# A feed-forward phase in 16 groups of two tiles instead of 8 groups of four

## The chip, the cores and the metric

One core of one Trainium2 chip. The number is the device time of one execution of the whole kernel in microseconds, the median of the runs shown; lower is better. Engine names: PE is TensorE (PEld its weight loads), DVE VectorE, ACT ScalarE, POOL GpSimd, SP SyncE.

## What is computed

The kernel is a two-layer perceiver block on x of 64 x 64 rows of 256 numbers. It has six sub-layers, each added to x: cross-attention with biases, a polynomial self-attention, a mixture of experts, a second cross-attention, a softmax self-attention, and last the feed-forward that is changed here. Cut to that one:

```python
def act_quant(x):            # one scale for each row
    scale = 127.0 / clip(max(abs(x), axis=-1), 1e-5)
    return clip(round(x * scale), -128, 127) / scale
# weight_quant: one scale for the matrix, values -1, 0, 1
h = act_quant(layernorm(x)) @ weight_quant(w1).T    # 256 -> 1024
h = depthwise_conv1d(h, conv_w, conv_b)             # 3 taps over the 64 rows of a sequence
h = silu(h)
x = x + act_quant(h) @ weight_quant(w2).T           # 1024 -> 256
```

## The kernel before, in words

X, the running sum, stays in SBUF as 32 tiles of 128 rows (two sequences of 64 rows each). The sub-layers are phases one behind another, each a block of five instruction streams, one for each engine, tied by counting semaphores. `feed_forward` (L2012) is the last but the output transfer.

It works on groups of G = 4 tiles, W = 512 columns, n = 8 groups. Its stream on each engine is `step(s, par)`, run by `tile_steps` for s = 0 to n + 3: steps 0 to 3 are written out, the middle ones are a loop of two steps a turn with counters in registers, the last four are written out. One step does pieces of five groups at once, in eight slots f = 0 to 7, one for each block of 128 hidden features:

- group s: statistics (L2177, L2181), 1/std on POOL (L2099, L2101), xn (L2187), its greatest absolute value and the scale (L2193 to L2201), rounding to xr (L2270), transposition (L2327) and xqT (L2243), and back_b, the scale spread over all partitions by a matmul with diagonal matrices (L2275, L2333, L2247).
- group s-1: for each f two bf16 matmuls w1 x xqT (L2296) into ps_h, h (L2152) on DVE, two float32 matmuls with diagonal matrices for the outer taps (L2304) into ps_y one slot later, y with the middle tap (L2160) two slots later, SiLU on ACT (L2252) three slots later. In f = 7 the peak over the first four feature blocks (L2169).
- group s-2: in f = 3 the peak over the other four and the maximum of both (L2169, L2174), four transposes of it (L2312), in f = 4 the greatest value of each row and scale2 (L2206 to L2214), four diagonals diag2 (L2264), in f = 5 the matmul L2318, in f = 6 scale_b (L2238). From there POOL multiplies (L2107) and rounds (L2115) y.
- group s-3: hq in bf16 on ACT (L2258).
- group s-4: the output matmuls (L2342), for each tile eight of 256 columns into ps_o[i % 2], and the update of X (L2219). PE does tiles 0 and 1 in f = 0 and tiles 2 and 3 in f = 1; before tile i it waits until X has been updated for tile i-2, since the buffer is the same (L2339). DVE updates tiles 0 and 1 in f = 1, 2 and 3 in f = 2.

Every engine works strictly in the order of its stream, so a wait holds up all that is written behind it. The order is written by hand. The PSUM buffers ps_h, ps_y and ps_o are double; ps_x and ps_b are single and serve two groups each in a step.

Of the kernel before, what the change touches and what calls it, by code (L numbers as in the profile page):

```python
# [28 lines left out]
ALU = mybir.AluOpType  # L29
# [1982 lines left out]
def feed_forward(nc, c, X, d):  # L2012
# [7 lines left out]

    G, n, F = 4, NT // 4, 1024
    FC = F // P
    W = G * P
    with ExitStack() as ctx:
# [93 lines left out]
        def _(dve):  # L2120
# [21 lines left out]
            def step(s, par):  # L2142
                q, last = s - 2, s - 4
                for f in range(FC):
                    g = s - 1
                    if live(g, n):

                        if f == 0:
                            dve.wait_ge(back_ready, g + 1)
                        dve.wait_ge(h_done, FC * g + f + 1)  # L2150
                        wait(dve, taps_done, FC * g + f - 3)
                        V.tensor_tensor(h[:, f % 4, :, 1:T + 1], ps_h[f % 2][:, :].rearrange("p (b t) -> p b t", t=T),  # L2152
                                        back_b[:, 1 - par, :].rearrange("p (b t) -> p b t", t=T), ALU.mult)\
                            .then_inc(h_ready, 1)
                    g, j = unit(s, f, 2)
                    if live(g, n):
                        yp = (par + 1 + (f < 2)) % 2
                        dve.wait_ge(taps_done, FC * g + j + 1)
                        wait(dve, hq_ready, FC * (g - 2) + j + 1)
                        V.scalar_tensor_tensor(y[:, yp, j, :].rearrange("p (b t) -> p b t", t=T),  # L2160
                                               h[:, j % 4, :, 1:T + 1], cw[:, j, 1:2],
                                               ps_y[j % 2][:, :].rearrange("p (b t) -> p b t", t=T),
                                               ALU.mult, ALU.add).then_inc(y_ready, 1)
                    g, half = (s - 1, 0) if f == 7 else (q, 1)
                    if f in (3, 7) and live(g, n):
# [37 lines left out]
                    if f == 4 and live(q, n):  # L2203
                        dve.wait_ge(peak_done, q + 1)
                        wait(dve, diag2_ready, q)
                        V.tensor_reduce(top2[:, :], ps_x[:, :].rearrange("p (i c) -> p i c", i=G), AX.X, ALU.max)\  # L2206
                            .then_inc(top2_ready, 1)
                        dve.wait_ge(top2_ready, 3 * q + 1)
                        V.tensor_scalar(top2[:, :], top2[:, :], 1e-5, None, ALU.max).then_inc(top2_ready, 1)
                        dve.wait_ge(top2_ready, 3 * q + 2)  # L2210
                        V.reciprocal(scale2[:, :], top2[:, :]).then_inc(top2_ready, 1)
                        dve.wait_ge(top2_ready, 3 * q + 3)
                        V.tensor_scalar(scale2[:, :], scale2[:, :], 127.0, None, ALU.mult)
                        V.tensor_scalar(back2[:, par, :], top2[:, :], w_mean[:, 1:2], 1.0 / 127, ALU.mult, ALU.mult)\  # L2214
                            .then_inc(scale2_ready, 1)
                    if f in (1, 2) and live(last, n):
                        for i in (2 * f - 2, 2 * f - 1):
                            dve.wait_ge(o_done, G * last + i + 1)
                            V.scalar_tensor_tensor(X[:, last * G + i, :], ps_o[i % 2][:, 0:E], back2[:, par, i:i + 1],  # L2219
                                                   X[:, last * G + i, :], ALU.mult, ALU.add).then_inc(x_updated, 1)  # L2220
            tile_steps(dve, step, n=n, lag=4)

        @block.scalar
        def _(act):
            act.wait_ge(consts_set, 4)
            act.wait_ge(loaded, 16 * n_loads)
            for i, t in enumerate((0, 2)):
                for j in range(FC):
                    ins = nc.scalar.activation(tap[:, i, j, :], c.ident[:, :], ACT.Copy, scale=cw[:, j, t:t + 1])
            ins.then_inc(tap_set, 1)  # L2230

            def step(s, par):
                q = s - 2
                for f in range(FC):
                    if f == 6 and live(q, n):
                        act.wait_ge(scale_done, q + 1)
                        wait(act, scaled, FC * (q - 1))
                        nc.scalar.activation(scale_b[:, par, :], ps_b[:, :], ACT.Copy).then_inc(scale_ready, 1)  # L2238
                    if f == 6 and live(s, n):
                        wait(act, h_done, FC * (s - 1))  # L2240
                        for k in range(KC):
                            act.wait_ge(xT_done, KC * s + k + 1)
                            nc.scalar.activation(xqT[:, par, k, :], ps_x[:, :], ACT.Identity,  # L2243
                                                 bias=rounding[:, 1:2]).then_inc(xqT_ready, 1)
                        act.wait_ge(back_done, s + 1)
                        wait(act, h_ready, FC * (s - 1))
                        nc.scalar.activation(back_b[:, par, :], ps_b[:, :], ACT.Copy).then_inc(back_ready, 1)  # L2247
# [12 lines left out]
                    if f == 4 and live(q, n):  # L2260
                        act.wait_ge(scale2_ready, q + 1)
                        wait(act, scale_done, q)
                        for i in range(G):
                            ins = nc.scalar.activation(diag2[:, i, :], c.ident[:, :], ACT.Copy, scale=scale2[:, i:i + 1])  # L2264
                        ins.then_inc(diag2_ready, 1)
                    if f == 5 and live(s, n):
                        act.wait_ge(scale1_ready, s + 1)
                        wait(act, xT_done, KC * s)
                        for i in range(G):
                            ins = nc.scalar.activation(xr[:, i, :], xn[:, i, :], ACT.Identity, bias=rounding[:, 0:1],  # L2270
                                                       scale=scale1[:, i:i + 1])
                        ins.then_inc(xr_ready, 1)
                        wait(act, back_done, s)
                        for i in range(G):
                            ins = nc.scalar.activation(diag1[:, i, :], c.ident[:, :], ACT.Copy, scale=back1[:, i:i + 1])  # L2275
                        ins.then_inc(diag1_ready, 1)
            tile_steps(act, step, n=n, lag=4)

        @block.tensor
        def _(pe):  # L2280
# [6 lines left out]
            def step(s, par):  # L2287
                q, last = s - 2, s - 4
                for f in range(FC):
                    g = s - 1  # L2290
                    if live(g, n):
# [1 line left out]
                            pe.wait_ge(xqT_ready, KC * g + KC)  # L2293
                        wait(pe, h_ready, FC * g + f - 1)
                        for k in range(KC):
                            mm = nc.tensor.matmul(ps_h[f % 2][:, :], w1[:, k, f * P:(f + 1) * P],  # L2296
                                                  xqT[:, 1 - par, k, :], start=(k == 0), stop=(k == KC - 1))
                        mm.then_inc(h_done, 1)
                    g, j = unit(s, f, 1)
                    if live(g, n):  # L2300
                        pe.wait_ge(h_ready, FC * g + j + 1)
                        wait(pe, y_ready, FC * g + j - 1)
                        for i in range(2):
                            mm = nc.tensor.matmul(ps_y[j % 2][:, :], tap[:, i, j, :],  # L2304
                                                  h[:, j % 4, :, 2 * i:2 * i + T], start=(i == 0), stop=(i == 1))
                        mm.then_inc(taps_done, 1)
                    if f == 3 and live(q, n):
# [7 lines left out]
                    if f == 5 and live(q, n):  # L2315
                        pe.wait_ge(diag2_ready, q + 1)
                        pe.wait_ge(back_ready, q + 2 if not isinstance(q, int) else min(n, q + 2))
                        nc.tensor.matmul(ps_b[:, :], ones[:, :], diag2[:, :, :].rearrange("p i t -> p (i t)"),  # L2318
                                         start=True, stop=True).then_inc(scale_done, 1)
                    if f == 6 and live(s, n):  # L2320
                        pe.wait_ge(xr_ready, s + 1)
# [11 lines left out]
                        nc.tensor.matmul(ps_b[:, :], ones[:, :], diag1[:, :, :].rearrange("p i t -> p (i t)"),  # L2333
                                         start=True, stop=True).then_inc(back_done, 1)
                    if f < 2 and live(last, n):
                        pe.wait_ge(hq_ready, FC * last + FC)
                        for i in (2 * f, 2 * f + 1):
                            if isinstance(s, int) or f == 1:
                                wait(pe, x_updated, G * last + i - 1)  # L2339

# [133 lines left out]
```

## Time and profile before

| | us |
|---|---|
| median of 3 runs | 2681.48 (2681.24 to 2689.95) |
| the profiled execution | 2684.85 |
| its span | 2683.1 |
| feed-forward, first statistics to last update of X | 318.2 |
| mean granted clock of PE over the span | 0.915 |

Over the whole span PE is busy 82%, DVE 56%, ACT 38% and POOL 34%. A row of the timeline reads: start, length, engine, line, operation, output<-inputs, sizes, how often, and in brackets how long the engine stood idle before it and who released it. "f32 x4" are four instructions merged. A row of the stages reads: stretch, its length, busy time of PE, PEld, DVE, ACT and POOL with the number of instructions, the mean clock that PE was granted as a share of full speed, the DMA share and GB/s. A row of the groups reads: line, engine, operation, sizes, count | busy us, mean ns of one | idle time before and who ended it.

### The profile page before, as it was taken

What the parts mean: (1) busy time and instruction counts of PE and PEld (TensorE: products, weight loads), DVE (VectorE), ACT (ScalarE), POOL (GpSimd) and SP (SyncE); (2) the same over time, 40 slices, a digit from 0 to 9 for tenths busy, and PEclk for the clock granted to TensorE, in tenths of its full rate; (3) what the DMA queues carried; (4) which work ended last, traced back from release to release, by engine and by line L of the source; (5) the groups of instructions that cost most, each with busy time, mean ns of one, the idle gap of its engine ahead of it and who ended that gap; (6) DMA issues with size and microseconds to landing.
All of it is one profiled execution on the core that took longest, in us unless ns stands there. A gap on an engine that the chain in (4) does not pass through costs nothing. (4 is left out here: it accounts for less than half of the span.)

```text
span 2683.1 us, 58677 instructions
## 1 busy us (share of the span) xinstructions
PE 2207.0 (82%) x19450; PEld 1620.2 (60%) x19463; DVE 1490.4 (56%) x4214; ACT 1012.8 (38%) x2135; POOL 900.2 (34%) x1082
## 2 busy tenths in 40 slices
PE   4999999999789963399999999976776888567774
PEld 4777777777679963156555555545555777533332
DVE  4666666666566657422233333326664777567763
ACT  3665666566444410011122222212223555334442
POOL 3444444444211112377000000017763333205555
PEclk9999999999888875699999999998997999878986
DMA  3000001000033311454122222225541000100001
GB/s 119 29 27 26 26 26 34 28 26 26 17 115 98 98 37 37 166 185 172 51 76 76 78 76 77 77 99 149 162 144 23 9 8 8 37 0 1 0 0 63
DMA packets 164872, 168.38 MB, mean 63 GB/s; under 512 B 81841, under 2 KB 139954, under 8 KB 163506
## 3 DMA queue, kind: packets, MB, share of 16 engines
q1 hardware_dynamic: 124162, 83.27, 10.7%
q0 software_dynamic: 17152, 52.45, 5.9%
q10 hardware_dynamic: 23472, 31.54, 3.4%
q8 instruction: 51, 0.84, 0.1%
q14 instruction: 35, 0.29, 0.0%
HBM read 100.09 MB, written 62.91 MB: 61 GB/s over the span
## 5 line engine op out<-in xcount | busy, mean ns | idle before, releaser
L1921 POOL DMA_INDIRECT xb_expert_y<-expert_outs,moe_slot x128 | 125.7, 982 | 561.3 <-POOLq L76 526.1
L1812 PE MATMUL ex_ps_h<-moew_w,ex_xT 128*128 x576 | 287.5, 622 | 20.7 <-DVE ex_xT L1870 9.8
L427 ACT ACTIVATE xa_prob<-xa_neg_s,xa_neg_max 128x256 f32<-128x256 f32 x512 | 224.4, 499 | 130.3 <-DVE xa_neg_max L314 130.3
L1865 DVE TENSOR_TENSOR ex_g<-ex_act_g,ex_ps_h 128x256 f32<-128x256 f32 x144 | 60.7, 421 | 311.4 <-ACT ex_act_g L1845 311.4
L314 DVE CUSTOM_DVE_ANT_0 xa_neg_s<-xa_ps_s,xa_mask 128x256 f32<-128x256 f32 x512 | 191.1, 421 | 39.0 <-PE xa_ps_s L481 24.9
L434 ACT ACTIVATE xa_probT<-xa_ps_s 128x512 f32<-128x512 f32 x256 | 151.9, 593 | 58.5 <-PE xa_ps_s L492 57.0
L510 PE MATMUL xa_ps_o<-xa_v,xa_probT 128*64 128x34 f32 x4096 | 172.9, 229 | 0.2 <-ACT xa_probT L434 0.2
L1812 PEld LDWEIGHTS ex_ps_h<-moew_w,ex_xT 128*128 128x128 f32 x576 | 98.0, 190 | 123.8 <-issue 123.8
L510 PEld LDWEIGHTS xa_ps_o<-xa_v,xa_probT 128*64 128x64 f32 x4096 | 143.9, 140 | 47.8 <-issue 40.0
L492 PE MATMUL xa_ps_s<-g_ident,xa_prob 128*128 128x128 f32 x1024 | 163.9, 283 | 2.8 <-ACT xa_prob L427 2.4
L1845 ACT ACTIVATE ex_act_g<-ex_ps_h 128x256 f32<-128x256 f32 x144 | 55.2, 383 | 293.9 <-PE ex_ps_h L1812 293.9
L1826 PE MATMUL ex_ps_y<-moew_w,ex_gT 128*128 x576 | 148.4, 380 | 1.2 <-DVE ex_gT L1875 1.2
L270 POOL TENSOR_TENSOR xa_qz<-xa_q,xa_in_pair 128x256 fp32r<-128x256 f32 x128 | 74.5, 613 | 197.5 <-DVE xa_q L362 197.5
L1676 POOL DMA_INDIRECT expert_rows<-sh_xn,sh_idx x128 | 123.1, 962 | 51.3 <-issue 38.5
L2304 PE MATMUL ff_ps_y<-ff_h,ff_tap 128*128 128x512 f32 x256 | 133.2, 647 | 7.4 <-DVE ff_y L2160 7.4
L492 PEld LDWEIGHTS xa_ps_s<-g_ident,xa_prob 128*128 128x128 f32 x1024 | 112.5, 141 | 10.9 <-ACT xa_prob L427 3.7
L1945 PE MATMUL xb_ps_g<-xb_ctx_rows 128*128 128x256 f32 x512 | 117.8, 384 | 0.0
L2107 POOL TENSOR_TENSOR ff_y<-ff_y,ff_scale_b 128x512 f32<-128x512 f32 x64 | 82.2, 1286 | 101.9 <-ACT ff_scale_b L2238 101.9
L1080 POOL TENSOR_TENSOR sa_shifted<-sa_masked,sa_top 128x512 f32<-128x512 f32 x64 | 68.1, 1064 | 125.6 <-DVE sa_top L1099 125.6
L1826 PEld LDWEIGHTS ex_ps_y<-moew_w,ex_gT 128*128 128x128 f32 x576 | 98.3, 190 | 9.6 <-issue 2.1
L1945 PEld LDWEIGHTS xb_ps_g<-xb_ctx_rows 128*128 128x128 f32 x512 | 95.9, 192 | 12.6 <-issue 0.4
L1849 ACT ACTIVATE ex_y<-ex_ps_y 128x256 f32<-128x256 f32 x144 | 55.2, 383 | 105.5 <-PE ex_ps_y L1826 105.5
(298 smaller groups left out, 4911.7 us busy)
## 6 DMA issues: line engine op xcount, KB each, us to landing
expert_rows<-sa_zero POOLq DMA_DIRECT2D x16, 1152.0 KB, 5.6
ex_xg<-expert_rows SPq DMA_DIRECT2D x144, 128.0 KB, 2.0
expert_outs<-ex_y ACTq DMA_DIRECT2D x144, 128.0 KB, 1.7
xa_ctxT<-in_ctxT_dram SPq DMA_DIRECT2D x32, 512.0 KB, 3.5
xb_ctx_rows<-in_ctx_rows_dram SPq DMA_DIRECT2D x32, 512.0 KB, 4.1
moew_w<-in_moe_w_dram ACTq DMA_DIRECT2D x8, 1024.0 KB, 5.5
g_x<-in_x_dram SPq DMA_DIRECT2D x4, 1024.0 KB, 9.9
sa_v<-sa_vs SPq DMA_DIRECT2D x128, 32.0 KB, 2.2
```

The source lines that it names most:

```text
L314: ins = nc.vector.tensor_tensor_reduce(neg_s[:, u % 2, g, :], ps_s[j][:, g * S:(g + 1) * S], mask[:, b, :], -1.0, 3e38, ALU.add, ALU.min, ...
L427: ins = nc.scalar.activation(prob[:, u % 2, i, :], neg_s[:, u % 2, i, :], ACT.Exp, bias=neg_max[:, u % 2, i:i + 1], scale=-1.0)
L434: nc.scalar.activation(probT[:, u % 2, :, :, :].rearrange("p i c t -> p (i c t)"), ps_s[u % 4][:, :], ACT.Copy).then_inc(t_ready, 1)
L492: mm = nc.tensor.transpose(ps_s[u % 4][:, k:k + P], prob[:, u % 2, g, ch * P:(ch + 1) * P], c.ident[:, :])
L510: mm = nc.tensor.matmul(ps_o[b][rows, q * 2 * D1:(q + 1) * 2 * D1], probT[:, u % 2, g, ch, rows], v[:, ap, 2 * b + ch, 2 * q:2 * q + 2, :] ...
L1676: nc.gpsimd.indirect_dma_start(c.xg_dram[:, :], bass.IndirectOffsetOnAxis(ap=idx[:, par, TOP * i + k:TOP * i + k + 1], axis=0), xn[:, par, ...
L1812: mm = nc.tensor.matmul(ps_h[1 - par][:, :], xT[:, 1 - par, k, :], c.w1[:, own, k, :], start=(k == 0), stop=(k == KC - 1))
L1826: mm = nc.tensor.matmul(ps_y[1 - par][:, 0:E], gT[:, 1 - par, k, :], c.w2[:, own, k, :], start=(k == 0), stop=(k == KC - 1))
L1921: nc.gpsimd.indirect_dma_start(expert_y[:, s % 4, k, :], None, c.y_dram[:, :], bass.IndirectOffsetOnAxis(ap=c.slot[:, s, k:k + 1], axis=0))\
L1945: mm = nc.tensor.matmul(ps_g[q % 2][b][:, g * E:(g + 1) * E], ctx_rows[:, q, 2 * b + k, g * P:(g + 1) * P], ctx_rows[:, q, 2 * b + k, :], ...
L2107: nc.gpsimd.tensor_tensor(y[:, gp, j, :], y[:, gp, j, :], scale_b[:, gp, :], ALU.mult)\
L2304: mm = nc.tensor.matmul(ps_y[j % 2][:, :], tap[:, i, j, :], h[:, j % 4, :, 2 * i:2 * i + T], start=(i == 0), stop=(i == 1))
```

## The change

G becomes 2 and n becomes 16: W is 256 columns, and all tiles of SBUF follow W. The PSUM tiles stay 512 wide, and only their first W columns are used. One output tile is made in f = 0 and one in f = 1 (i = f), and DVE updates X for tile 0 in f = 1 and tile 1 in f = 2 (i = f - 1). The slots, their order, the semaphores and the waits' formulas stay. There are 20 steps instead of 12: four written out, a loop of six turns of two steps instead of two turns, four written out. Nothing is changed outside `feed_forward`.

```diff
-    G, n, F = 4, NT // 4, 1024
+    G, n, F = 2, NT // 2, 1024
...
-                        V.tensor_tensor(h[:, f % 4, :, 1:T + 1], ps_h[f % 2][:, :].rearrange("p (b t) -> p b t", t=T),
+                        V.tensor_tensor(h[:, f % 4, :, 1:T + 1], ps_h[f % 2][:, 0:W].rearrange("p (b t) -> p b t", t=T),
...
                     if f in (1, 2) and live(last, n):
-                        for i in (2 * f - 2, 2 * f - 1):
+                        for i in (f - 1,):
                             dve.wait_ge(o_done, G * last + i + 1)
...
                     if f < 2 and live(last, n):
                         pe.wait_ge(hq_ready, FC * last + FC)
-                        for i in (2 * f, 2 * f + 1):
+                        for i in (f,):
                             if isinstance(s, int) or f == 1:
                                 wait(pe, x_updated, G * last + i - 1)
```

The other edits put `0:W` in place of `:` for ps_y in L2160 and L2304, ps_x in L2206 and L2243, ps_b in L2238, L2247, L2318 and L2333, and ps_h in L2296.

## Rows read from the trace of the kernel before

**Rows 1.** The page, part 4: the chain that ended last, by line

```profile
PE ff_ps_y L2304 1%; DVE ff_peak L2169 1%; PE ff_ps_h L2296 1%; DVE ff_y L2160 1%; PE ff_ps_o L2342 1%; ACT ff_xr L2270 0%; POOL ff_y L2107 0%; DVE ff_h L2152 0%; DVE ff_top L2193 0%; POOL ff_y L2115 0%; PE ff_ps_b L2333 0%; PE ff_ps_x L2312 0%; PE ff_ps_b L2318 0%; DVE ff_stats L2177 0%; PE ff_ps_x L2327 0%
```

**Rows 2.** Busy time by stretch of the feed-forward: fill, step 3, steps 4 to 8, drain

```profile
2350.13:2400.16 50.03, 33.22 (x86) 14.41 (x88) 32.70 (x67) 18.70 (x33) 3.79 (x6) 0.81 0.00 0
2400.16:2432.06 31.90, 24.32 (x63) 10.62 (x64) 24.27 (x41) 15.36 (x29) 15.05 (x15) 0.87 0.00 1
2432.06:2609.60 177.54, 135.97 (x472) 67.14 (x480) 131.58 (x217) 84.83 (x160) 97.98 (x91) 0.91 0.00 0
2609.60:2668.30 58.70, 32.51 (x135) 18.79 (x136) 24.27 (x36) 20.80 (x35) 37.09 (x33) 0.72 0.00 0
```

**Rows 3.** Timeline of two neighbouring steps, 2454 to 2486 us

```profile
2454.63 0.70 DVE L2152 TENSOR_TENSOR ff_h<-ff_ps_h,ff_back_b 128x512 f32<-128x512 f32 x1
2455.23 0.76 DVE L2160 SCALAR_TENSOR_TENSOR ff_y<-ff_h,ff_cw,ff_ps_y 128x512 f32<-128x512 f32 x1
...
2459.26 1.92 PE L2342 MATMUL ff_ps_o<-ff_w,ff_hq 128*128 128x256 bf16 x16 [1.18 <-DVE g_x L2219]
...
2461.74 0.69 DVE L2152 TENSOR_TENSOR ff_h<-ff_ps_h,ff_back_b 128x512 f32<-128x512 f32 x1 [2.14 <-PE ff_ps_h L2296]
...
2468.79 1.05 DVE L2174 TENSOR_TENSOR ff_peak<-ff_peak 128x512 f32<-128x512 f32 x1
...
2471.97 0.69 DVE L2152 TENSOR_TENSOR ff_h<-ff_ps_h,ff_back_b 128x512 f32<-128x512 f32 x1 [0.84 <-PE ff_ps_h L2296]
...
2476.58 1.28 ACT L2264 ACTIVATE ff_diag<-g_ident,ff_scale 128x128 f32<-128x128 f32 x4 [10.06 <-DVE ff_back L2214]
...
2477.91 1.13 PE L2318 MATMUL ff_ps_b<-ff_diag,ff_ones 128*128 128x512 f32 x2 [0.39 <-ACT ff_diag L2264]
...
2485.31 0.69 DVE L2152 TENSOR_TENSOR ff_h<-ff_ps_h,ff_back_b 128x512 f32<-128x512 f32 x1 [4.45 <-PE ff_ps_h L2296]
```

**Rows 4.** The chain in order of time: start, length, what

```profile
2504.43 1.06 DVE ff_peak L2174
...
2520.58 1.72 PE ff_ps_y L2304 x4
```

**Rows 5.** Timeline of DVE in the first cross-attention, 256-wide instructions

```profile
505.57 0.42 DVE L314 CUSTOM_DVE_ANT_0 xa_neg_s<-xa_ps_s,xa_mask 128x256 f32<-128x256 f32 x1
...
505.91 0.42 DVE L314 CUSTOM_DVE_ANT_0 xa_neg_s<-xa_ps_s,xa_mask 128x256 f32<-128x256 f32 x1
```

**Rows 6.** Groups of instructions by shape, feed-forward

```profile
L2169 DVE TENSOR_REDUCE ff_peak<-ff_y 128x512 f32<-128x2048 f32 x16 | 59.6, 3725 | 0.0
...
L2252 ACT ACTIVATE ff_y<-ff_y,ff_cb 128x512 f32<-128x512 f32 x64 | 45.6, 716 | 61.5 <-DVE ff_y L2160 61.5
...
L2193 DVE TENSOR_REDUCE ff_top<-ff_xn 128x4 f32<-128x1024 f32 x8 | 9.7, 1213 | 0.0
```

**Rows 7.** Groups of instructions by shape, other phases, 256 columns

```profile
L1945 PE MATMUL xb_ps_g<-xb_ctx_rows 128*128 128x256 f32 x512 | 117.8, 384 | 0.0
...
L1845 ACT ACTIVATE ex_act_g<-ex_ps_h 128x256 f32<-128x256 f32 x144 | 55.2, 383 | 293.9 <-PE ex_ps_h L1812 293.9
```

**Rows 8.** The chain in order of time, POOL's last pairs: first, and what follows them

```profile
2642.29 1.26 POOL ff_y L2107
...
2660.08 1.01 POOLq L2026
```

**Rows 9.** Busy time by stretch: two at low clock, one idle in the gram phase

```profile
2390.00:2393.00 3.00, 3.00 (x6) 1.23 (x5) 1.98 (x8) 0.72 (x1) 1.13 (x2) 0.50 0.00 0
2468.60:2475.20 6.60, 5.23 (x11) 2.55 (x12) 5.62 (x14) 0.00 (x0) 0.69 (x1) 0.50 0.00 0
1904.24:1906.00 1.76, 0.00 (x1) 0.01 (x1) 1.09 (x4) 0.00 (x0) 1.28 (x3) 1.00 0.84 179
```

**Rows 10.** Who waited for whom in the feed-forward: us, times, longest

```profile
PE ff_ps_x L2312 <- DVE ff_peak L2174: 36.3, 8, 5.6
```

**Rows 11.** Timeline of PE, the tap matmuls before that low stretch

```profile
2389.00 2.83 PE L2304 MATMUL ff_ps_y<-ff_h,ff_tap 128*128 128x512 f32 x4 [2.08 <-DVE ff_y L2160]
```

More of the change, by code:

```diff
@@ L2161, in step @@
                                                h[:, j % 4, :, 1:T + 1], cw[:, j, 1:2],
-                                               ps_y[j % 2][:, :].rearrange("p (b t) -> p b t", t=T),
+                                               ps_y[j % 2][:, 0:W].rearrange("p (b t) -> p b t", t=T),
                                                ALU.mult, ALU.add).then_inc(y_ready, 1)
@@ L2205, in step @@
                         wait(dve, diag2_ready, q)
-                        V.tensor_reduce(top2[:, :], ps_x[:, :].rearrange("p (i c) -> p i c", i=G), AX.X, ALU.max)\
+                        V.tensor_reduce(top2[:, :], ps_x[:, 0:W].rearrange("p (i c) -> p i c", i=G), AX.X, ALU.max)\
                             .then_inc(top2_ready, 1)
@@ L2237, in step @@
                         wait(act, scaled, FC * (q - 1))
-                        nc.scalar.activation(scale_b[:, par, :], ps_b[:, :], ACT.Copy).then_inc(scale_ready, 1)
+                        nc.scalar.activation(scale_b[:, par, :], ps_b[:, 0:W], ACT.Copy).then_inc(scale_ready, 1)
                     if f == 6 and live(s, n):
@@ L2242, in step @@
                             act.wait_ge(xT_done, KC * s + k + 1)
-                            nc.scalar.activation(xqT[:, par, k, :], ps_x[:, :], ACT.Identity,
+                            nc.scalar.activation(xqT[:, par, k, :], ps_x[:, 0:W], ACT.Identity,
                                                  bias=rounding[:, 1:2]).then_inc(xqT_ready, 1)
@@ L2246, in step @@
                         wait(act, h_ready, FC * (s - 1))
-                        nc.scalar.activation(back_b[:, par, :], ps_b[:, :], ACT.Copy).then_inc(back_ready, 1)
+                        nc.scalar.activation(back_b[:, par, :], ps_b[:, 0:W], ACT.Copy).then_inc(back_ready, 1)
                     g, j = unit(s, f, 3)
@@ L2295, in step @@
                         for k in range(KC):
-                            mm = nc.tensor.matmul(ps_h[f % 2][:, :], w1[:, k, f * P:(f + 1) * P],
+                            mm = nc.tensor.matmul(ps_h[f % 2][:, 0:W], w1[:, k, f * P:(f + 1) * P],
                                                   xqT[:, 1 - par, k, :], start=(k == 0), stop=(k == KC - 1))
@@ L2303, in step @@
                         for i in range(2):
-                            mm = nc.tensor.matmul(ps_y[j % 2][:, :], tap[:, i, j, :],
+                            mm = nc.tensor.matmul(ps_y[j % 2][:, 0:W], tap[:, i, j, :],
                                                   h[:, j % 4, :, 2 * i:2 * i + T], start=(i == 0), stop=(i == 1))
@@ L2317, in step @@
                         pe.wait_ge(back_ready, q + 2 if not isinstance(q, int) else min(n, q + 2))
-                        nc.tensor.matmul(ps_b[:, :], ones[:, :], diag2[:, :, :].rearrange("p i t -> p (i t)"),
+                        nc.tensor.matmul(ps_b[:, 0:W], ones[:, :], diag2[:, :, :].rearrange("p i t -> p (i t)"),
                                          start=True, stop=True).then_inc(scale_done, 1)
@@ L2332, in step @@
                         wait(pe, back_ready, s)
-                        nc.tensor.matmul(ps_b[:, :], ones[:, :], diag1[:, :, :].rearrange("p i t -> p (i t)"),
+                        nc.tensor.matmul(ps_b[:, 0:W], ones[:, :], diag1[:, :, :].rearrange("p i t -> p (i t)"),
                                          start=True, stop=True).then_inc(back_done, 1)
```

## The prediction

> **What bounds the kernel now.** I read the page's chain first [rows 1]: the work that ended last runs through the feed-forward, and no single engine carries it. PE's tap matmuls (L2304), DVE's peak reduction (L2169), PE's L2296 and DVE's L2160 share it. The change touches this phase only, so I take the phase's own clock: from its first statistics at 2350.13 us to its last update of X at 2668.3, 318.2 us of the profiled span.
>
> Next I cut that stretch at the ends of the peak reduction of f=3 [rows 2]: 50.0 us until step 2's, 31.9 for step 3, 177.5 for five more steps (35.5 each), 58.7 of drain. 318.2 less eight steps of 35.5 is 34: all that filling and draining cost beyond eight full steps. In each of the five steps PE is busy 27.2 us, DVE 26.3, POOL 19.6, ACT 17.0. Nobody is full; the step is a ring of hand-overs.
>
> The timeline of a loop step shows the ring [rows 3]. I count from one start of L2174 (2468.79) to the next (2504.43 [rows 4]), 35.64 us, in three parts:
> - A, 9.12 us, to the scale matmul L2318 (2477.91). The reader should see L2174, then four transposes and L2296 until the h of f=4 can start (3.18); then h, y, the top of xn, the second top and their small operations until ACT gets the scale of diag2 (4.61); then four diagonals (1.33).
> - B, 7.40 us, to the h of f=7 (2485.31): on ACT two activations, four xr, four diag1, scale_b, two xqT, with PE's transposes between, then L2333 and L2296.
> - C, the other 19.12 us, mostly DVE. Its later pieces are seen a step earlier in the rows: from h of f=0 to PE's third output tile 4.63, in which PE stood 1.18 us for g_x; from there to h of f=2 2.48, in which DVE stood 2.14 for PE; f=2, f=3 and the peak 7.05. The remainder, h, y and peak of f=7, is 4.96.
>
> **What the change does to the sum.** Twice the steps, half the columns. If a step halved exactly, 16 steps of 17.8 would cost what 8 of 35.5 do, and fill and drain would halve: 17 us gained. But every microsecond of a step that doesn't halve is paid 14 to 16 times, so the result hangs on one number, the length of the new step; break-even is about 1.1 over half.
>
> What halves: the counts of transposes, diagonals, xr, statistics, normalisations, output tiles. What has a fixed part: every instruction that stays and gets narrower. What of it is exposed comes from start-to-start times. DVE at 256 columns takes 0.42 us and the next starts after 0.34 [rows 5]; h at 512 takes 0.70 and y starts after 0.60 [rows 3]. So 256 columns are 0.27 and 0.07 stays: h 0.33, y 0.39 from start to start. ACT takes 0.716 at 512 [rows 6] and 0.383 at 256, there read from PSUM [rows 7]: I take 0.21 off every wide ACT instruction. PE does 512 instructions of 256 columns in 117.8 us, 0.23 each [rows 7], against 0.43 for 512 [rows 4]: the four of L2304 take 0.92 for 1.72, L2296 0.22 to 0.24. The peak reduction (3.725 [rows 6]) does the same for half as many outputs: 1.87. L2193 loses 512 of its elements, 0.53 of 1.21 [rows 6]. The ten small operations and their waits don't shrink.
>
> A: L2174 0.60 (bounds 0.42, the clean 256-wide row, and 0.9: its 1.05 at 512 lies 0.35 over h's, beside POOL's work, and may keep that); 0.12 hand-over, two transposes 0.55 and L2296 0.43, these at the low clock: 1.70 for 3.18. Then 4.61 less 0.27 each for h, y and the second top and 0.53 for the first: 3.27. Diagonals 1.33 - 0.64 = 0.69. A = 5.66; half would be 4.56. PE's tap matmuls of f=4 and 5 hid this chain; they now end before it, and PE waits some 2 us for diag2.
>
> B: 7.40 less two activations 0.42, two xr 0.98, two diag1 0.59, scale_b 0.21, xqT 0.21, transposes 0.33, L2333 0.43, L2296 0.22: 4.0 (half 3.70). PE's own path from L2318, 0.70 + 0.24 + 0.92 = 1.9, ends with the xr and stays hidden at full clock.
>
> C: 0.72 and 1.87 for the 4.96. Then the removed wait: with one output tile in f=0 and one in f=1, each has its own PSUM buffer, read out a step ago, so PE no longer waits for g_x. Late next is y of f=0, for which the taps of f=1 wait: h 0.33, y 0.47, hand-over 0.12, taps 1.05, L2342 0.96 (eight of the sixteen that took 1.92 [rows 3]), L2296 and hand-over 0.28: 3.2 for 7.11. DVE's own work in it, two h, two y, two statistics, two aggregates and one g_x, is 2.65, covered. Then 3.8 for 7.05 (DVE 3.72, but PE's taps and L2296 before h of f=3 add 0.1). C = 9.6 (half 9.56).
>
> **Step: 5.66 + 4.0 + 9.6 = 19.3 us,** 1.5 over half. POOL needs some 10.5 of it (eight pairs of 1.2, rstd 1.0), ACT about 11: covered. The steps issue no DMA; SP's queue holds only the output, unchanged.
>
> Fill: the same subtractions give 8.6 us to the first h, 12.6 for the rest of step 1, 6.6 for step 2 to its peak: 27.8 for 50.0. Step 3 17.2. Loop steps 4 to 15: 12 x 19.3 = 231.6. Step 16, without new statistics, 18.5. Drain 58.7 to 32: the last eight POOL pairs, 17.8 us [rows 8], to 9.6, the rest near half. Sum 27.8 + 17.2 + 231.6 + 18.5 + 32 = 327.1 against 318.2: +8.9. The profiled execution took 2684.85 us and would become 2693.8; the median of the runs shown is 2681.48, 3.4 lower, and I put the change on that: 2690.
>
> **A rule of the skill against the rows.** The rows: an instruction's fixed part is about 0.15 us, but only 0.07 of it delays the next DVE instruction [rows 3, 5]. The Trainium skill ("VectorE: DVE Perf Modes", The TRN2 errata) says that SBUF latency is exposed between instructions, that many small tiles pay it once each, and advises tiles of 512 elements or more; the change goes from 512 to 256. By that rule the sum would be about +26 instead of +8.9. No row shows how far it holds behind this phase's waits; rival 2 is what it would do here.
>
> **Rivals.**
> 1. *The low clock reaches into part B (slower).* After the peak reduction PE stands at half clock for 6.6 us [rows 9]. The transposes will follow about 2.4 us of idle PE instead of 4.5 (36.3 in 8 waits [rows 10]). Rows go both ways: 2.08 us of waiting [rows 11] was followed by 3 us at 0.50, while 1.76 us in the gram phase left the clock at 1.00 [rows 9]. My sum has the low clock on the transposes and the L2296 of f=4 only. It decides from where the low stretch outlasts the diag2 wait, some 5 us after the transposes start: then L2318, L2296 and L2304 take 3.3 instead of 1.9 and the next transposes 0.3 more, +1.7 a step, 14 steps, +24: 2714. If the clock never falls, -0.4 a step: 2684, within the forecast.
> 2. *Short instructions cost their full length (slower).* DVE's next instruction would start 0.42 to 0.47 after a 256-wide one, since each h and y pair carries four waits. Against it: 0.34 in the attention phase, though with fewer waits. Some 14 such instructions lie on the path: +1.2 a step, +17: 2707.
> 3. *The peak reduction more than halves (faster).* L2169 takes 1.8 ns for each element it reads, L2193 1.2 [rows 6]. If its stride of 2 KB is the reason, 1 KB may be cheaper: two reductions save up to 0.65 each, 1.3 a step, -21 in all, so -12: 2669. Against: reducing four elements at a time may itself be the cost, and that stays.
> 4. *The groups are not really halved.* Loop, waits and buffers of the diff all follow G; I give it 0.02.
>
> **Chances.** Forecast 0.46 (2690, own range 2682 to 2700, a seventh of it past the bound); rival 1 0.20; rival 2 0.13; rival 3 0.12; rival 4 0.02; unnamed 0.07, mostly slower. 0.5%, 13.4 us, is about what a measurement of this kernel can tell from no change: below 2668 is faster, above 2695 slower. Faster: the better half of rival 3 and some of the unnamed, 0.10. Slower: 0.07 + 0.20 + 0.12 + 0.02 = 0.41. Same: the rest, 0.49. The range runs from rival 3's value to just past rival 1's: 2668 to 2718.
>
> **What would show it.** Start to start of L2174 in the loop near 19.3 (18.9 with full clock, over 20.5 in rivals 1 and 2); h to y 0.33 (rival 2: 0.42); L2169 near 1.87 (rival 3: 1.2); PE waiting about 2 us for ff_diag before L2318 in each step; no wait of ff_ps_o for g_x; clock of a loop step over 0.85 (rival 1: 0.75); fill 28, drain 32. Steps of 18 or less, or of 21 or more, would prove the walk wrong.

## The result, and the profile after

| | before | after |
|---|---|---|
| median of 4 runs, us | 2682.56 (2681.24 to 2689.95) | 2713.20 (2709.76 to 2717.56) |
| the profiled execution | 2684.85 | 2709.76 |
| its span | 2683.1 | 2707.6 |
| feed-forward, first statistics to last update of X | 318.2 | 346.5 |

The ratio is 1.0109, with a 95% interval of 1.0084 to 1.0134: slower by 1.1%, inside the range, but 23 us above the forecast of 2690. The phase took 28.3 us more; the sum had said 8.9. (The phase also began 3.8 us earlier in the profiled execution, which is why its total differs by 24.9 only; the medians differ by 30.6.) The times and medians below leave out one far slower execution each of e1 (3817 us, granted clock 0.55) and of e3 (6493 us).

The chain of work by line, answering [rows 1]:

```profile
PE ff_ps_y L2304 2%; DVE ff_peak L2169 1%; DVE ff_y L2160 1%; PE ff_ps_o L2342 1%; PE ff_ps_h L2296 1%; DVE ff_xn L2187 0%; PE ff_ps_b L2318 0%; DVE ff_h L2152 0%; PE ff_ps_x L2327 0%; DVE ff_top L2193 0%; PE ff_ps_b L2333 0%; ACT ff_xqT L2243 0%; DMA ff_cb<-in_ff_cb_dram 0%; DVE ff_top L2206 0%; ACT ff_diag L2264 0%
```

It is still a ring of hand-overs, with two changes: L2304 has gone from 1% to 2%, and xn (L2187), which was on no list before, is now on it. Both turn out to matter.

The busy time by stretch, answering [rows 2]: fill, step 3, steps 4 to 16, drain, cut at the starts of L2174.

```profile
2346.31:2375.82 29.51, 18.71 (x80) 12.68 (x80) 18.57 (x51) 12.00 (x25) 2.79 (x6) 0.79 0.00 1
2375.82:2395.02 19.20, 14.25 (x58) 10.03 (x58) 13.95 (x36) 9.58 (x23) 8.36 (x14) 0.82 0.00 0
2395.02:2659.48 264.46, 198.81 (x962) 139.21 (x962) 199.53 (x477) 139.15 (x339) 147.71 (x236) 0.90 0.00 0
2659.48:2692.78 33.30, 17.64 (x84) 11.44 (x84) 14.23 (x30) 13.63 (x31) 20.91 (x33) 0.75 0.00 1
```

The third row is twelve loop steps, 245.0 us, and step 16, 19.5. Twelve loop steps are 20.41 us each, not 19.3. But they are not alike: three took 19.6, nine took 20.6 to 20.8. The timeline of a short step, start to start of L2174, to be laid beside [rows 3]:

```profile
2435.21 0.54 DVE L2174 TENSOR_TENSOR ff_peak<-ff_peak 128x256 f32<-128x256 f32 x1
2435.67 1.43 DVE L2187 TENSOR_SCALAR ff_xn<-g_x,ff_mv,ff_rstd 128x256 f32 x2
2435.88 0.43 PE L2312 MATMUL ff_ps_x<-g_ident,ff_peak 128*128 128x128 f32 x2 [2.41 <-DVE ff_peak L2174]
2436.15 0.38 PE L2296 MATMUL ff_ps_h<-ff_xqT,ff_w 128*128 128x256 bf16 x2
...
2437.02 0.41 DVE L2152 TENSOR_TENSOR ff_h<-ff_ps_h,ff_back_b 128x256 f32<-128x256 f32 x1
2437.36 0.47 DVE L2160 SCALAR_TENSOR_TENSOR ff_y<-ff_h,ff_cw,ff_ps_y 128x256 f32<-128x256 f32 x1
2437.75 0.67 DVE L2193 TENSOR_REDUCE ff_top<-ff_xn 128x2 f32<-128x512 f32 x1
...
2440.25 0.69 ACT L2264 ACTIVATE ff_diag<-g_ident,ff_scale 128x128 f32<-128x128 f32 x2 [5.50 <-DVE ff_back L2214]
...
2441.00 0.70 PE L2318 MATMUL ff_ps_b<-ff_diag,ff_ones 128*128 128x256 f32 x2 [0.98 <-ACT ff_diag L2264]
...
2445.11 0.42 DVE L2152 TENSOR_TENSOR ff_h<-ff_ps_h,ff_back_b 128x256 f32<-128x256 f32 x1 [2.35 <-PE ff_ps_h L2296]
```

The parts can be read off: A 5.79 us (2435.21 to 2441.00), B 4.11 (to 2445.11), C 9.69 (to the next L2174, 2454.80). The sum had 5.66, 4.0 and 9.6. H to y is 0.34 and y to the next instruction 0.39.

The next step is a long one. Its part A is 5.79 again (2454.80 to 2460.59), its C 9.67, but its B is 5.22:

```profile
2460.59 0.96 PE L2318 MATMUL ff_ps_b<-ff_diag,ff_ones 128*128 128x256 f32 x2 [1.93 <-ACT ff_diag L2264]
...
2461.35 0.63 PE L2296 MATMUL ff_ps_h<-ff_xqT,ff_w 128*128 128x256 bf16 x2
...
2461.77 1.91 PE L2304 MATMUL ff_ps_y<-ff_h,ff_tap 128*128 128x256 f32 x4
...
2463.48 0.63 PE L2327 MATMUL ff_ps_x<-g_ident,ff_xr 128*128 128x128 f32 x2
...
2465.81 0.42 DVE L2152 TENSOR_TENSOR ff_h<-ff_ps_h,ff_back_b 128x256 f32<-128x256 f32 x1 [2.98 <-PE ff_ps_h L2296]
```

L2304 takes 1.91 here against 1.03 for the same four instructions at full clock. The granted clock of two stretches, one in each step:

```profile
2436.40:2440.40 4.00, 3.61 (x12) 2.01 (x10) 3.79 (x15) 0.15 (x1) 0.55 (x1) 0.57 0.00 0
2460.40:2464.00 3.60, 3.41 (x10) 2.28 (x10) 0.94 (x3) 2.77 (x8) 0.75 (x2) 0.57 0.00 0
```

In the short step the clock is at its low level (1.2 GHz) for most of the stretch, while PE has nothing urgent: it would wait for diag2 afterwards (0.98 us instead of 1.93). In the long step the clock is full in that place and low behind the diag2 wait, and there L2318, L2296, the taps and the transposes of xr stand one behind another on the way to the h of f = 7.

Six of the nine long steps are like this one: the low stretch starts 5.5 to 6.1 us after the step's start, about when diag2 comes (5.8). The other three (those of 2415, 2517 and 2619 us) have a single longer one, from the first taps (1.9) to 8.7, across the wait:

```profile
2519.00:2525.60 6.60, 5.62 (x15) 3.42 (x14) 4.35 (x16) 3.33 (x9) 0.14 (x1) 0.50 0.00 0
```

The order is not random. From 2435.21 on the steps are 19.59, 20.68, 20.83, 20.70 and 20.60, and then the same five again within 0.02.

The groups of instructions by shape of the phase after, answering [rows 6], with two more:

```profile
L2252 ACT ACTIVATE ff_y<-ff_y,ff_cb 128x256 f32<-128x256 f32 x128 | 63.8, 501 | 42.5 <-DVE ff_y L2160 42.4
L2169 DVE TENSOR_REDUCE ff_peak<-ff_y 128x256 f32<-128x1024 f32 x32 | 61.9, 1936 | 0.1
L2187 DVE TENSOR_SCALAR ff_xn<-g_x,ff_mv,ff_rstd 128x256 f32 x24 | 17.2, 755 | 0.0
...
L2193 DVE TENSOR_REDUCE ff_top<-ff_xn 128x2 f32<-128x512 f32 x16 | 10.8, 674 | 0.0
...
L2174 DVE TENSOR_TENSOR ff_peak<-ff_peak 128x256 f32<-128x256 f32 x16 | 8.5, 534 | 0.6
```

The same view of the kernel before has for xn, in its last four groups:

```profile
L2187 DVE TENSOR_SCALAR ff_xn<-g_x,ff_mv,ff_rstd 128x256 f32 x16 | 5.5, 401 | 0.0
```

Xn is made of instructions that the change doesn't touch, 256 columns before and after, and one went from 401 to 755 ns on average. What stands beside it on POOL, in the timeline of before (a step that starts at 2468.79) and of after (one that starts at 2454.80):

```profile
2468.25 1.04 POOL L2115 TENSOR_TENSOR ff_y<-ff_y,ff_rounding 128x512 f32<-128x512 f32 x1
```

```profile
2455.01 0.91 POOL L2107 TENSOR_TENSOR ff_y<-ff_y,ff_scale_b 128x256 f32<-128x256 f32 x1
...
2455.89 0.66 POOL L2115 TENSOR_TENSOR ff_y<-ff_y,ff_rounding 128x256 f32<-128x256 f32 x1
```

POOL's last pair ended 0.5 us behind the start of the step before, and 1.75 us behind it now. The kernel before had one step in which POOL ran later still, the first of its loop (start 2432.08, and with 36.7 us its longest). There a pair stood at 2432.87 to 2435.63, and the first two of four xn took 1.36 and 1.12 us:

```profile
2433.39 3.05 DVE L2187 TENSOR_SCALAR ff_xn<-g_x,ff_mv,ff_rstd 128x256 f32<-128x256 f32 x4
```

So the sign of this cost was already in the trace of before. And who waited for whom on PE:

```profile
PE ff_ps_x L2312 <- DVE ff_peak L2174: 39.2, 16, 3.3
PE ff_ps_b L2318 <- ACT ff_diag L2264: 23.5, 16, 2.6
```

The wait for g_x before the output matmuls, 6.4 us in 5 waits before, is gone altogether.

### The profile page after: what moved, and what is told of

Its sections match the earlier page's. It is cut to its first block and busy times, and to the rows that moved or that the text cites. A ratio compares the mean times of both kernels' runs of the same rounds, so it can differ in the third digit from the quotient of the medians.

```text
span 2707.6 us, 60913 instructions
## 1 busy us (share of the span) xinstructions
PE 2225.1 (82%) x19878; PEld 1678.0 (62%) x19879; DVE 1522.5 (56%) x4446; ACT 1048.3 (39%) x2295; POOL 929.1 (34%) x1226
## 5 line engine op out<-in xcount | busy, mean ns | idle before, releaser
L314 DVE CUSTOM_DVE_ANT_0 xa_neg_s<-xa_ps_s,xa_mask 128x256 f32<-128x256 f32 x512 | 190.9, 421 | 36.7 <-PE xa_ps_s L481 23.7
L2304 PE MATMUL ff_ps_y<-ff_h,ff_tap 128*128 128x256 f32 x512 | 155.2, 430 | 10.1 <-DVE ff_y L2160 9.8
L2107 POOL TENSOR_TENSOR ff_y<-ff_y,ff_scale_b 128x256 f32<-128x256 f32 x128 | 95.9, 749 | 105.4 <-ACT ff_scale_b L2238 105.4
L2304 PEld LDWEIGHTS ff_ps_y<-ff_h,ff_tap 128*128 128x128 f32 x512 | 97.6, 212 | 35.8 <-DVE ff_h L2152 16.6
```

Source lines behind the costliest of these rows:

```text
L314: ins = nc.vector.tensor_tensor_reduce(neg_s[:, u % 2, g, :], ps_s[j][:, g * S:(g + 1) * S], mask[:, b, :], -1.0, 3e38, ALU.add, ALU.min, ...
L2107: nc.gpsimd.tensor_tensor(y[:, gp, j, :], y[:, gp, j, :], scale_b[:, gp, :], ALU.mult)\
L2304: mm = nc.tensor.matmul(ps_y[j % 2][:, 0:W], tap[:, i, j, :], h[:, j % 4, :, 2 * i:2 * i + T], start=(i == 0), stop=(i == 1))
```

## The experiments

Two theories stood at the start. **A:** the walk is right in kind, and the excess is the low clock in part B (rival 1, smaller than priced). **B:** narrow instructions cost more than the walk had, in the removed cover or in the fixed parts, and the clock is a side effect. The kernel before was run again beside each batch; its medians were 2683.85, 2681.41 and 2682.26 us. "Steps" are from start to start of L2174 in the loop. The fillers are bf16 matmuls of weights into ps_b, overwritten before anything reads it. They shift later line numbers: L2310 and L2321 are the fillers, L2315 the transposes, L2323 the scale matmul, L2347 the output matmul.

**1. Groups of two, clock held up (e1_warm).**

```diff
                     if f == 3 and live(q, n):
+                        pe.wait_ge(back_ready, ...)
+                        for _ in range(16):
+                            nc.tensor.matmul(ps_b[:, 0:256], w2[:, 0, 0:P], w1[:, 0, 0:256], start=True, stop=True)
                         pe.wait_ge(peak_ready, 3 * q + 3)
...
                     if f == 5 and live(q, n):
-                        pe.wait_ge(diag2_ready, q + 1)
                         pe.wait_ge(back_ready, ...)
+                        for _ in range(12):
+                            nc.tensor.matmul(ps_b[:, 0:256], w2[:, 0, 0:P], w1[:, 0, 0:256], start=True, stop=True)
+                        pe.wait_ge(diag2_ready, q + 1)
```

> The kernel after, with filler matmuls of 256 columns on TensorE that nothing reads: 16 before it waits for the peak, 12 before it waits for diag2. They fit into its idle time. Theory A (the low clock that reaches the scale matmul costs 1.1 us in 9 of the 12 loop steps, and a part of the extra time of the change): granted clock 1.00 through the loop, every loop step 19.4 to 19.6 us, 10 to 13 us less than the kernel after, so 2700 to 2703. Theory B (the clock is only a companion, the steps are long because of fixed parts): loop steps stay at 20.4 on average, 2713. If the fillers themselves hold up the transposes: longer than 2713.

Measured 2700.33 us, ratio to before 1.0057 (1.0037 to 1.0077). The twelve loop steps as one stretch:

```profile
2397.74:2632.82 235.08, 200.60 (x1224) 148.64 (x1224) 184.97 (x444) 127.65 (x313) 135.84 (x218) 1.00 0.00 0
```

Clock 1.00, and every step 19.58 to 19.61. PE is busier than in the changed kernel (200.6 us of 235.1 against 183.9 of 245.0), and the kernel is 12.9 us faster. This is the clock's share, shown. What is left, +16.5 on the median and 334.3 against 318.2 for the phase, is not the clock.

**2. The removed wait put back (e2_one_buffer, and with the clock held e10_one_buffer_warm).**

```diff
-                            V.scalar_tensor_tensor(X[:, last * G + i, :], ps_o[i % 2][:, 0:E], back2[:, par, i:i + 1],
+                            V.scalar_tensor_tensor(X[:, last * G + i, :], ps_o[0][:, 0:E], back2[:, par, i:i + 1],
...
-                                wait(pe, x_updated, G * last + i - 1)
+                                wait(pe, x_updated, G * last + i)
...
-                                mm = nc.tensor.matmul(ps_o[i % 2][:, 0:E], hq[:, par, k, i * P:(i + 1) * P],
+                                mm = nc.tensor.matmul(ps_o[0][:, 0:E], hq[:, par, k, i * P:(i + 1) * P],
```

> The kernel after, with both output tiles of a step in one PSUM buffer, so that TensorE waits in f=1 until X has been updated for the first tile, as it did with four tiles. If the removed wait was worth what the prediction took (0.4 us a step against half of before): L2342 of f=1 starts 0.8 us later, steps +0.8 us, some 13 us more than after: 2726. If another wait had long covered it: no change, 2713.

Measured 2718.0 us, 1.0128 (1.0107 to 1.0148): +4.8 on the changed kernel, between the two expectations, and it settled little. The wait was there (0.7 us in a step), but the steps ran from 20.5 to 21.6 in a new pattern, since moving a wait also moved the low clock. So the pair was run once more with the fillers:

> Groups of two, both output tiles in one PSUM buffer, so that PE waits for g_x again, with the fillers of e1_warm so that the clock stays at 1.00. The price of the removed wait without the clock in it, against e1_warm (2700.4, steps 19.6). Theory A: the wait of 0.7 us is paid in full in each of 16 steps: steps 20.3 to 20.4, total 2711 to 2713. Theory B: part of it is covered by DVE's or ACT's own work behind it, 0.3 a step: steps 19.9, total 2705.

Measured 2710.62, 1.0101 (1.0085 to 1.0116), steps 20.38 to 20.41 (the loop's first 20.49), 0.81 above e1_warm's, at clock 1.00. Timeline of one step:

```profile
2469.59 1.04 PE L2347 MATMUL ff_ps_o<-ff_w,ff_hq 128*128 128x256 bf16 x8
2472.56 0.45 DVE L2219 SCALAR_TENSOR_TENSOR g_x<-ff_ps_o,ff_back,g_x 128x256 f32 x1
...
2473.06 1.05 PE L2347 MATMUL ff_ps_o<-ff_w,ff_hq 128*128 128x256 bf16 x8 [0.71 <-DVE g_x L2219]
```

PE waits 0.71 us for the update of X and the step grows by 0.81: the wait lies on the ring with its full length. The walk had put the release of this wait into part C, and it is real. It also shows why e2 couldn't be read: where the clock alternates, a change of 0.8 us is drowned by a pattern of 1.1.

**3. POOL's rounding cut short (e3_no_rounding).** L2115 rounds 8 of the 256 columns and leaves the others as they are, so POOL has less to do.

```diff
-                        nc.gpsimd.tensor_tensor(y[:, gp, j, :], y[:, gp, j, :],
-                                                rounding[:, 0:1].to_broadcast([P, W]), ALU.add).then_inc(rounded, 1)
+                        nc.gpsimd.tensor_tensor(y[:, gp, j, 0:8], y[:, gp, j, 0:8],
+                                                rounding[:, 0:1].to_broadcast([P, 8]), ALU.add).then_inc(rounded, 1)
```

> Leaves out most of the computation of GpSimd's rounding: L2115 works on 8 columns instead of 256, so the outputs are not rounded there. GpSimd then has done its pairs before the peak ends. If GpSimd's traffic is what stretches L2174 (0.54 instead of 0.42) and the second xn (0.95 for two instead of 0.66), h of f=4 starts 0.3 to 0.4 us earlier: steps -0.3, about 5 us less, more in the drain (8 x 0.5 = 4 us less): 2704. If the reading is wrong and xn is slow of itself: L2187 stays at 755 ns and only the drain is shorter: 2709.

Measured 2696.60, 1.0044 (1.003 to 1.0057): 16.6 faster than the changed kernel, more than either expectation. The groups by shape:

```profile
L2187 DVE TENSOR_SCALAR ff_xn<-g_x,ff_mv,ff_rstd 128x256 f32 x24 | 8.8, 406 | 0.0
...
L2174 DVE TENSOR_TENSOR ff_peak<-ff_peak 128x256 f32<-128x256 f32 x16 | 6.9, 434 | 0.6
```

755 went to 406 ns and 534 to 434 with no edit of DVE: it was POOL's work beside them. The shortest steps went from 19.58 to 19.02, so what two xn and L2174 lose beside POOL, 0.8 us, costs the step 0.56; the h of f = 4 starts 1.25 after the step's start instead of 1.81. In the profiled execution the phase is 14.4 us shorter: 4.4 in the drain and 9.5 in the loop, of which twelve times 0.56 is 6.7. The other 2.8 go with a kinder clock pattern (steps of 19.0 to 20.85, 19.63 on average); this run can't tell whether that comes from POOL or from the moved waits.

**4. DVE's two chains of f = 4 exchanged (e4_order).** In f = 4 DVE finds scale1 of group s (L2193 to L2201) and then scale2 of group q (L2206 to L2214). Only the second is what PE waits for.

```diff
+                    if f == 4 and live(q, n):
+                        dve.wait_ge(peak_done, q + 1)
...
                     if f == 4 and live(s, n):
                         dve.wait_ge(xn_ready, s + 1)
...
-                    if f == 4 and live(q, n):
-                        dve.wait_ge(peak_done, q + 1)
...
```

> The kernel after, with the order on VectorE turned in f=4: first group q's chain (L2206 to L2214), then group s's (L2193 to L2202); nothing else. If the chain of small operations before diag2 is the bound of part A, the scale matmul starts 1.3 us earlier, TensorE's idle time before it nearly goes, and the clock with it: steps 18.3 to 18.6, 2682 to 2690. If part B's bound is the xr instead, which need group s's scale: only 0.3 us a step, 2708. If TensorE's own work bounds part A: no change.

Measured 2686.01, 1.001 (0.9997 to 1.0023): the first expectation, 27.2 faster than the changed kernel. Of the loss of 30.6 nothing is left that can be told from noise. The timeline (in this kernel L2193 to L2201 are group q's, since the text is exchanged too) and the loop as one stretch:

```profile
2441.48 0.41 DVE L2193 TENSOR_REDUCE ff_top<-ff_ps_x 128x2 f32<-128x256 f32 x1
...
2442.53 0.68 DVE L2206 TENSOR_REDUCE ff_top<-ff_xn 128x2 f32<-128x512 f32 x1
2442.66 0.69 ACT L2264 ACTIVATE ff_diag<-g_ident,ff_scale 128x128 f32<-128x128 f32 x2 [4.18 <-DVE ff_back L2201]
...
2443.41 0.70 PE L2318 MATMUL ff_ps_b<-ff_diag,ff_ones 128*128 128x256 f32 x2 [0.60 <-ACT ff_diag L2264]
```

```profile
2401.70:2624.50 222.80, 173.66 (x888) 124.65 (x888) 184.11 (x444) 129.37 (x313) 135.71 (x218) 0.94 0.00 0
```

Every step is now 18.55 to 18.66. The clock is still not full (0.94), but it costs nothing: eight of the twelve steps have a low stretch, always between the step's start and 5.5 us, where PE would otherwise wait, and they are no longer than the four without. So there are two separate gains, and the fillers tell them apart. With 16 fillers of e1's kind before the peak wait on top (e8_both):

> Groups of two, DVE's two chains of f=4 exchanged, and 16 filler matmuls (256 columns, read by nothing) before the wait for the peak of f=3. Theory A (once the chain to diag2 comes first, the low stretch falls where PE waits anyway): steps stay at 18.56, total 2683 to 2689, as with the exchange alone (2686.0). Theory B (the transposes and the L2296 of f=4 at low clock still cost 0.4 us a step, as the prediction had it): steps 18.15, total 2679 to 2681.

Measured 2685.75, 1.0015 (1.0004 to 1.0026); the twelve loop steps:

```profile
2394.97:2617.80 222.83, 185.41 (x1080) 135.46 (x1080) 183.85 (x444) 129.34 (x313) 135.84 (x218) 1.00 0.00 0
```

222.83 against 222.80 us with the clock at 1.00 instead of 0.94: theory A of that run. The exchange is worth 1.03 a step at full clock (19.59 to 18.56), and in the alternating pattern it takes the 0.82 of the clock as well.

**5. The same two edits in groups of four (e6_before_order, e5_before_warm, e7_before_both).** If narrow groups are what exposes the chain to diag2, the exchange should do little in the kernel before. E6 has the diff of e4, e5 has 18 fillers of 512 columns before the peak wait, e7 has both.

> The kernel before with group q's chain ahead of group s's on VectorE in f=4, the edit of e4_order. With four tiles, TensorE's tap matmuls at the low clock end only 0.4 us before diag2 comes, so the earlier chain should give 0.4 us a step at most: -3 us, 2680. If it gives 1.3 us or more a step as with two tiles (-10 us), then the chain, not TensorE, bounds part A in both, and the exposure isn't owed to the narrow groups.

Measured 2672.12, 0.9963 (0.9949 to 0.9977): the second expectation. Timeline of PE and ACT in one step:

```profile
2465.66 1.28 ACT L2264 ACTIVATE ff_diag<-g_ident,ff_scale 128x128 f32<-128x128 f32 x4 [7.50 <-DVE ff_back L2201]
...
2466.39 1.88 PE L2304 MATMUL ff_ps_y<-ff_h,ff_tap 128*128 128x512 f32 x4
...
2468.10 1.02 PE L2318 MATMUL ff_ps_b<-ff_diag,ff_ones 128*128 128x512 f32 x2
```

L2318 now starts straight behind the taps, without a wait (there is one such wait left in the whole phase): here PE's own work bounds part A. The five steps went from 35.5 to 33.7 on average, so the chain had bound groups of four as well, and my sentence that PE's taps "hid this chain" was wrong.

> The kernel before (groups of four), with 18 filler matmuls of 512 columns on TensorE before it waits for the peak, 3.9 us in its 4.5 us of idle time. If the low clock after the peak costs the kernel before too: transposes and L2296 0.85 us faster, steps 34.8 instead of 35.6, 5 to 8 us less than before in all, 2676. If everything behind the low clock is hidden by VectorE's chain there: no change.

Measured 2681.39, 0.9997 (0.9986 to 1.0007): the number of the second expectation, but not by its reason. PE in one of its steps:

```profile
2500.83 4.05 PE L2310 MATMUL ff_ps_b<-ff_w 128*128 128x512 bf16 x18
...
2512.56 1.13 PE L2321 MATMUL ff_ps_b<-ff_diag,ff_ones 128*128 128x512 f32 x2 [2.11 <-ACT ff_diag L2264]
...
2514.09 3.44 PE L2304 MATMUL ff_ps_y<-ff_h,ff_tap 128*128 128x512 f32 x4
```

Part A ran at full clock, so PE came earlier to the diag2 wait and stood there 2.11 us, and the clock fell behind that wait: the taps of part B took 3.44 instead of 1.88. Of the five steps two are like this (37.5 and 35.5 us). In the neighbouring ones the same wait of 2.11 left the clock at 1.00, and they took 34.75, 0.5 to 0.9 less than such steps before (35.3 and 35.6): near the first expectation's 0.85. So the low stretch of before was not harmless, and curing it made another in some steps, as narrowing the groups had done. In the profiled execution the phase is 4.2 us shorter (314.0); the medians don't show it.

> The kernel before with both edits, fillers and order. At full clock TensorE is through the taps of f=5 about 2.5 us earlier, and diag2 comes 1.9 us earlier: part A shorter by about 1.9 us, steps 33.7, -13 us, 2669: the two gains need each other, and four tiles a group are then faster than two in any form tried. If they only add (0.85 + 0.4 a step): 2674.

Measured 2667.08, 0.995 (0.9937 to 0.9962): the first expectation in the total, with steps of 32.9 instead of 33.7, and the fastest version of this study, ahead of both kernels. Four loop steps:

```profile
2428.86:2561.36 132.50, 115.61 (x450) 56.49 (x457) 105.39 (x180) 67.93 (x128) 78.31 (x74) 1.00 0.00 1
```

With e8 this makes the clean comparison of widths, both with the exchange and at clock 1.00: three of these steps are 32.9, half is 16.45, and two tiles take 18.56. So narrowing costs 2.1 us a step, with the wait for g_x that it removes and the traffic of POOL beside xn that it adds both in this number; the phase is 303.9 us in groups of four and 319.9 in groups of two.

**6. Groups of one tile (e9_one_tile, e11_one_tile_warm).** G = 1, n = 32, 128 columns, one output tile in f = 0 in a single buffer; e11 with 8 and 11 fillers at the two places of e1.

```diff
-    G, n, F = 2, NT // 2, 1024
+    G, n, F = 1, NT, 1024
...
-                    if f in (1, 2) and live(last, n):
+                    if f == 1 and live(last, n):
...
-                    if f < 2 and live(last, n):
+                    if f == 0 and live(last, n):
...
-                            if isinstance(s, int) or f == 1:
-                                wait(pe, x_updated, G * last + i - 1)
+                            if isinstance(s, int):
+                                wait(pe, x_updated, last)
```

> Groups of one tile, 32 groups, W = 128, one output tile in f=0; the rest as after. Steps of 35.5 us at 512 columns and 19.6 at 256 (full clock) give 15.9 us for 256 columns and 3.7 fixed. If a step is linear in its width: 11.7 us at 128, a fill of about 20 and a drain of about 20, in all about 32 x 11.7 + 20 = 394 instead of 318: 2755 to 2765. If the small operations become the bound of a longer part of the ring (part A cannot fall below some 4.5 us, and the low clock comes in every step): 12.5 us and more, 2785.

Measured 2842.74, 1.0596 (1.058 to 1.0613), steps 13.9 to 15.1: worse than both expectations.

> Groups of one tile with fillers before both waits (8 and 11 of 256 columns), so that the clock stays near 1.00. Theory A (a step is a fixed part and a part in proportion to its columns; 35.6 at four tiles and 19.6 at two give 3.6 + 8.0 a tile): steps 11.6, total 2755 to 2765. Theory B (what was slow in the one-tile steps of 14.5 us is mainly the hand-overs, not the clock): steps 13.3 to 14, total 2805 to 2830.

Measured 2773.93, 1.0339 (1.0322 to 1.0355), steps 12.37. A stretch of the loop of each, e9 first:

```profile
2398.10:2630.00 231.90, 175.71 (x1008) 146.97 (x1008) 150.23 (x528) 120.78 (x368) 112.94 (x288) 0.71 0.00 0
```

```profile
2390.75:2600.00 209.25, 176.50 (x1387) 141.57 (x1386) 158.79 (x560) 126.20 (x390) 119.31 (x304) 1.00 0.00 0
```

The fillers give back 69 us on the median, 64 of them in the phase (475.3 and 411.3): that is the clock's part of e9's loss, 0.71 in the loop with the waits unfilled. What remains is the fixed part: 12.37 is 2.6 over half of 19.59, where 11.6 had been expected and 13.3 was the rival's least. It is nearer to theory A, which was too kind by 0.8.

## Why the prediction was right and wrong

The direction and the range held; the likeliest case was not what happened. The time is that of rival 1 (2714) and its mechanism is at work, but that the number fits so well is luck: rival 1 had 24 us of low clock, and the runs show 12.2, with 7.2 more for sizes, and the rest in how the profiled executions lie to their medians.

- **"If a step halved exactly", the fixed parts.** Right in size. At full clock a step took 19.59 (e1) for 19.3 by the walk: A 5.79 for 5.66, B 4.11 for 4.0, C 9.69 for 9.6. Over twelve steps the 0.29 is 3.5 us. That A fits is partly luck. Its first piece was 1.70, with 0.98 for two transposes and L2296 at low clock; in the step shown from 2435 us both ran at full clock (0.43 and 0.38 us), and h starts 1.8 us after the step's start in every loop step, whatever the clock does. Without POOL beside xn this piece is 1.25 (e3). One term too long and one left out nearly cancelled.
- **0.07 us exposed per DVE instruction; h 0.33, y 0.39.** Right to 0.01 (0.34, 0.39). Rival 2 is refuted. What the Trainium skill says ("VectorE: DVE Perf Modes", The TRN2 errata), that the fixed cost is paid between instructions and that tiles of 512 are better, pointed the right way: 256 columns are dearer per element (h took 0.41 us for 256 columns and 0.69 for 512). But the size that I had put on it, 0.09 more per instruction in this phase, the rows don't show.
- **L2169 1.87.** Measured 1.936. Rival 3 is refuted: halving the stride made nothing cheaper; L2169 still takes 1.9 ns for each element.
- **L2174 0.60, and nothing for xn.** The first was close (0.53). The second is a term that failed: I counted POOL's eight pairs as "covered" by their sum (10.5 of 19.3) and didn't place them in the step. They begin with scale_b, 8.4 us after the step's start, and now run 1.75 us past the next start. Before, in all but one loop step, they ended half a microsecond behind it, before the first xn. So L2174 and now both xn run beside them, and the h of f = 4 waits for xn, not for PE: 1.81 after the start for 1.70 in the walk. E3 shows both the cause and its price, 0.56 a step.
- **The removed wait for g_x.** Right that it goes; e10 prices it at 0.81 a step in groups of two.
- **"PE waits some 2 us for diag2".** Right: 1.93 where the clock was full. "My sum has the low clock on the transposes and the L2296 of f=4 only" is the step that failed. In three steps of twelve the low stretch stayed in front of the wait and cost nothing; in nine it lay behind the diag2 wait, on the ring. Rival 1 put +1.7 on each of 14 steps, with the reason that the stretch that starts at the transposes would last past the wait. That is what three steps did, at a cost of 1.0; in six it starts only about when the wait ends, and costs 1.0 to 1.2. On average it is 0.82 a step, 9.9 us in the loop. The rest of the clock's 12.2 us (346.5 less e1's 334.3) is in the fill, 0.8, step 3, 1.3, and the drain, 0.2.
- **"PE's tap matmuls of f=4 and 5 hid this chain".** Wrong, as e6 showed, and the row had said so: L2318 stood 0.39 us for diag2 [rows 3]. It did no harm to the sum, which had the chain's own length on the path either way, but it hid the better edit: the order of DVE's work in f = 4 was worth 9 us before the change and 27 after it.
- **Fill, step 3, step 16, drain.** 29.5 for 27.8, 19.2 for 17.2, 19.5 for 18.5, 33.3 for 32. Without the clock: 28.7, 17.9, 19.5 and 33.1. The errors at full clock are 0.9, 0.7, 1.0 and 1.1; with the loop's 3.5 they make 7.2. The drain's POOL pairs, read in the chain of waits, were right (1.25 a pair), but before them and behind them little halves:

```profile
2687.51 0.58 POOLq L2026
2688.68 3.61 PE ff_ps_o L2342 x16
2692.31 0.48 DVE g_x L2219
```

The account: 8.9 forecast, 12.2 for the clock, 7.2 for sizes (half of it in the loop, the rest in fill, step 3, step 16 and drain), 28.3 measured in the phase.

Still open: why the clock alternates. In the changed kernel the pattern repeats every five steps, and in e9 every four (14.2, 13.9, 15.0, 14.9), so it isn't chance; but what sets it no run shows, and none changed one gap alone by small amounts.

## What to carry to other kernels

Before making the units of a hand-written pipeline narrower, price the step at the new width and multiply by the number of steps: fill and drain are saved once, while here every step paid 2.1 us over half. Place the other engines' work in the step instead of adding it up, since a queue that ends "within the step" can move beside the instructions on the ring. And a low clock costs only what stands behind it on the ring: before filling gaps, look at which wait the low stretch comes behind, and first bring forward the chain on which that wait depends (exchanging two independent chains gave back 27 of the 31 us that the change lost).

## What the runs showed of the hardware

- One low stretch can be exchanged for another. Filling the 5 us gap of PE in groups of four (e5) left the time at 0.9997 of before: the steps at full clock got 0.5 to 0.9 us shorter, but in two of five a wait for diag2 later in the step (2.11 and 2.49 us) was followed by half clock. With that wait nearly removed too (e7) the clock was 1.00 in the loop and the time 0.995.
- 2 us gaps of PE can be followed by half clock, or not, in the same kernel in neighbouring steps: after the 2.41 us wait for the peak the clock fell in the step of 2435 us and stayed full until the diag2 wait in that of 2454 us, and the same pattern came back five steps later. Filling most of two such gaps gave 1.00 throughout, with less time though with 38% more PE instructions in the loop (1224 matmuls for 888).
- DVE beside POOL, both on SBUF: an f32 TENSOR_SCALAR of 256 columns took 755 ns on average instead of 401 to 406, a TENSOR_TENSOR with both inputs in SBUF 534 instead of 434; h and y, which take one of their tensors from PSUM, kept their 0.41 and 0.47 us. The Trainium skill ("GPSIMD Engine Reference", Specifications) names DVE instructions with two SBUF inputs or in a two-port mode as those that contend. The trace agrees for the TENSOR_TENSOR; that the TENSOR_SCALAR, the one hit hardest, runs in such a mode no run here shows.
